# Reordering a software-pipelined loop: an x tile, a v1 sum, result copies and the gate's turn change places with roundings, packings and matmul blocks

## The reference, cut to what matters

```
y  = layernorm over channels(x)
ca = sigmoid(mlp(mean over positions(y)) + mlp(max over positions(y)))     # channel gate
y  = y * ca
s  = conv7x7([mean over channels(y), max over channels(y)])                # token gate
t  = x + y * sigmoid(s)                                                    # attention, then as tokens
h  = bitlinear(layernorm(t), w1)      # x rounded to 8 bits by its row maximum, w to -1, 0, 1
h  = gelu(h)
t  = t + bitlinear(h, w2)             # h rounded the same way
```

## Time and profile before

| | us |
|---|---|
| median of 3 runs | 318.17 (317.60 to 318.43) |
| the profiled execution, device time | 317.06 |
| its span in the profile | 315.2 |
| PE busy | 272.2 (86%) |
| DVE busy | 247.3 (78%) |
| ACT busy | 218.0 (69%) |
| POOL busy | 161.4 (51%) |

### The profile page before, as it was taken

One profiled execution on the slowest core, in us unless ns is written; L12 is line 12 of the kernel. 1 busy time (PEld: TensorE's weight loads), 2 busy tenths in 40 slices (PEclk: granted clock), 3 DMA queues, 4 the chain that ended last, 5 costly groups with the idle time before them and its releaser, 6 DMA issues.

```text
span 315.2 us, 5808 instructions
## 1 busy us (share of the span) xinstructions
PE 272.2 (86%) x1834; PEld 154.7 (49%) x1834; DVE 247.3 (78%) x558; ACT 218.0 (69%) x442; POOL 161.4 (51%) x256
## 2 busy tenths in 40 slices
PE   2557768496999999999999999999999998999974
PEld 2344645363455355635563556355636553554431
DVE  0756979879699969896989698969896988798410
ACT  2287398478486877687768776877687758777731
POOL 7404355316855385538553855385538553455410
PEclk9755758879699999999999999999999999999998
DMA  5899400003073049403840384049405630263493
GB/s 133 308 380 423 156 1 2 0 0 65 5 166 70 8 62 231 105 6 63 225 111 6 61 223 113 5 65 224 113 3 66 166 71 15 54 168 74 79 215 100
DMA packets 71077, 34.19 MB, mean 108 GB/s; under 512 B 52040, under 2 KB 68424, under 8 KB 70536
## 3 DMA queue, kind: packets, MB, share of 16 engines
q1 hardware_dynamic: 69384, 32.78, 41.5%
q10 hardware_dynamic: 1664, 1.05, 1.2%
HBM read 14.94 MB, written 6.29 MB: 67 GB/s over the span
## 4 chain that ended last, share of the span: by engine, by line
PE 52%; DVE 15%; POOL 13%; issue 8%; ACT 7%; DMA 3%; SPq 1%; ACTq 0%; POOLq 0%; DVEq 0%
PE ps_o L1153 17%; PE ps_h L1142 9%; PE ps_t L1142 9%; POOL v L451 5%; PE front L1073 4%; POOL w_room L474 3%; PE front L1063 3%; PE ps_t L1184 2%; POOL rs L445 2%; DVE pv L782 2%; ACT junk L520 2%; PE small L1089 2%; DVE w_room L884 2%; DVE t L814 2%; PE front L1162 2%
## 5 line engine op out<-in xcount | busy, mean ns | idle before, releaser
L1153 PE MATMUL ps_o<-w2T,hq 128*128 128x512 f16 x384 | 92.7, 380 | 1.2 <-DMA hq<-w_raw 1.2
L474 POOL TENSOR_SCALAR w_room<-w_room,q 128x1024 f32<-128x1024 f32 x48 | 59.3, 1247 | 54.3 <-DVE q L851 54.3
L841 DVE TENSOR_REDUCE amax<-w_room 128x1 f32<-128x1024 f32 (+1 forms) x48 | 57.2, 1208 | 2.2 <-ACT w_room L520 2.2
L1153 PEld LDWEIGHTS ps_o<-w2T,hq 128*128 128x128 f16 x384 | 35.4, 98 | 37.3 <-issue 3.6
L1142 PE MATMUL ps_h<-w1T,xq 128*128 128x512 f16 x208 | 52.3, 394 | 1.1 <-ACT xq L520 0.8
L520 ACT ACTIVATE w_raw<-w_room 128x1024 f16<-128x1024 f16 x48 | 50.1, 1048 | 0.6 <-POOL w_room L474 0.6
L520 ACT ACTIVATE w_room<-ps_h,s 128x512 f32<-128x512 f32 x52 | 35.0, 689 | 13.0 <-PE ps_h L1142 11.9
L1142 PE MATMUL ps_t<-w1T,xq 128*128 128x512 f16 x176 | 43.3, 384 | 0.0
L520 ACT ACTIVATE w_room<-ps_t,s 128x512 f32<-128x512 f32 x44 | 30.2, 687 | 8.4 <-PE ps_t L1142 8.3
L520 ACT ACTIVATE junk_m<-front 128x192 bf16<-128x192 f32 x64 | 20.5, 329 | 17.8 <-DVE pooled L757 17.7
L1142 PEld LDWEIGHTS ps_h<-w1T,xq 128*128 128x128 f16 x208 | 19.2, 100 | 23.2 <-issue 2.4
(11 more groups left out here) (121 smaller groups left out, 459.5 us busy)
## 6 DMA issues: line engine op xcount, KB each, us to landing
out<-w_room SPq DMA_DIRECT2D x16, 384.0 KB, 3.4
x_in<-in_x SPq DMA_DIRECT2D x14, 384.0 KB, 5.6
w_room<-in_L_ffn_w SPq DMA_DIRECT2D x4, 1024.0 KB, 8.7
w_raw<-in_L_ffn_w SPq DMA_DIRECT2D x4, 1024.0 KB, 12.1
x_in<-in_x ACTq DMA_DIRECT2D x2, 384.0 KB, 3.7
hq<-w_raw SPq DMA_TRANSPOSE x48, 3.2
fc_raw<-in_L_conv_fc_w ACTq DMA_DIRECT2D x2, 128.0 KB, 4.2
taps_rev<-in_L_conv_sa_w SPq DMA_DIRECT2D x2, 0.2 KB
```

Source lines behind the costliest of these rows:

```text
L474: pool.tensor_scalar(part, part, q2[tile.par][:, 0:1], MAGIC, ALU.mult, ALU.add).then_inc(g_rounded, 1)
L841: chain.mark(dve.tensor_reduce(amax2[:, i:i + 1], w1_room[:, first + i * F // 2:first + (i + 1) * F // 2 + i], AX.X, ALU.max, apply_absolu ...
L1153: last = pe.matmul(ps_o[:, :], hq[tile.par][:, k, :], w2T[:, k, :], start=(k == 0), stop=(k == NF - 1))
```

## The change

Four functions of the loop are reordered. No arithmetic is added or removed. One wait is added.

- POOL: `normalise1(fresh, 2)` moves from the end of the body to ahead of the last `round_g`, that of tile (nxt, 1), directly behind `normalise1(fresh, 0, 1)`.
- PE: `turn_x(fresh, 2)` moves ahead of `turn_xq(nxt, 2)` and the last quarter of `ffn_out(pair, 2)`. `turn_ca(att)` moves from behind the third block of `ffn_in(nxt, 1)` to behind the second.
- ACT: `pack_g` now packs one half at a time. At the body's start the second half of (pair, 1) goes behind `token_mean(att, 0)`. In the middle the second half of (pair, 2) goes behind `token_mean(att, 3)`. At the end `copy_out(pair, 1)` goes ahead of `sum_channels(att, 2)`, `copy_x(fresh, 2)` ahead of `copy_xq(nxt, 2)`, and the second half of (nxt, 0) to the very end. `copy_caT` moves one block of `gelu` forward.
- ACT: `gelu` waits before block 2 until the packings of the tile two before are done.

```
@@ POOL body
                     if turn and s == NT - 1:
                         normalise1(pair.plus(3), 0, 1)
+                        normalise1(pair.plus(3), 2)
                     if normalise or s < NT - 2:
                         round_g(Tile(pair, s + 2))
-                if turn:
-                    normalise1(pair.plus(3), 2)
@@ ACT gelu
+                    if b == 2:
+                        wait(act, g16_ready, tile.at(2, -2))
@@ ACT body
-                pack_g(Tile(pair, 1), Tile(pair.plus(-1), 2) if pair.c > 0 else None, OUT_BANK[0])
+                pack_g(Tile(pair, 1), 0)
+                if pair.c > 0:
+                    copy_out(Tile(pair.plus(-1), 2), OUT_BANK[0])
                 if attend:
                     token_mean(att, 0, V1_BANK[0])
+                pack_g(Tile(pair, 1), 1)
+                if attend:
                     token_mean(att, 1, V1_BANK[1])
...
-                pack_g(Tile(pair, 2), Tile(pair, 0), OUT_BANK[1])
+                pack_g(Tile(pair, 2), 0)
+                copy_out(Tile(pair, 0), OUT_BANK[1])
                 if attend:
                     token_mean(att, 3, V1_BANK[3])
+                pack_g(Tile(pair, 2), 1)
...
-                    gelu(Tile(nxt, 1), blocks=(0, 1, 2))
+                    gelu(Tile(nxt, 1), blocks=(0, 1))
                 if attend:
                     copy_caT(att)
                 if normalise:
-                    gelu(Tile(nxt, 1), blocks=(3,))
+                    gelu(Tile(nxt, 1), blocks=(2, 3))
                 if attend:
                     sum_channels(Tile(att, 0))
                     sum_channels(Tile(att, 1))
                 if normalise:
-                    pack_g(Tile(nxt, 0), halves=(0,))
+                    pack_g(Tile(nxt, 0), 0)
+                copy_out(Tile(pair, 1), OUT_BANK[2])
                 if attend:
                     sum_channels(Tile(att, 2))
-                copy_out(Tile(pair, 1), OUT_BANK[2])
-                if normalise:
-                    pack_g(Tile(nxt, 0), halves=(1,))
-                if normalise:
-                    copy_xq(Tile(nxt, 2), XQ_BANK[2])
                 if turn:
                     copy_x(Tile(fresh, 2), X_BANK[2])
+                if normalise:
+                    copy_xq(Tile(nxt, 2), XQ_BANK[2])
+                    pack_g(Tile(nxt, 0), 1)
@@ PE body
-                    ffn_in(Tile(nxt, 1), blocks=(0, 1, 2))
+                    ffn_in(Tile(nxt, 1), blocks=(0, 1))
                 if attend:
                     turn_ca(att)
                 if normalise:
-                    ffn_in(Tile(nxt, 1), blocks=(3,))
+                    ffn_in(Tile(nxt, 1), blocks=(2, 3))
...
                 ffn_out(Tile(pair, 2), (1, 2))
+                if turn:
+                    b = turn_x(Tile(fresh, 2), X_BANK[2], b)
                 if normalise:
                     a = turn_xq(Tile(nxt, 2), XQ_BANK[2], a)
                 ffn_out(Tile(pair, 2), (3,))
-                if turn:
-                    b = turn_x(Tile(fresh, 2), X_BANK[2], b)
```

More of the change, by code:

```diff
@@ L575, in gelu, with pack_g @@
                          scale=s1[tile.pair.par][:, tile.s:tile.s + 1])
-            def pack_g(tile, out_tile=None, out_bank=None, halves=range(2)):
+            def pack_g(tile, half):
                 if tile.at() < 2:
                     act.wait_ge(w_turned, 10)
[L582 to L588, removed]
+                cols = slice(half * F // 2, (half + 1) * F // 2)
+                wait(act, g_rounded, tile.at(2, half + 1))
+                wait(act, h_turned[tile.par][half], tile.turns(-1))
+                copy(g16[tile.par][:, cols], low_halves(g[tile.par][:, cols]), g16_ready, bias=-F16_ZERO)
             def copy_out(tile, bank):
@@ L655, in _ @@
             gelu(Tile(pair0, 1), None, h_start, (2, 3))
-            pack_g(Tile(pair0, 0))
+            pack_g(Tile(pair0, 0), 0)
+            pack_g(Tile(pair0, 0), 1)
             copy_x(Tile(pair2, 0), 1)
@@ L697, in body @@
                 if normalise:
-                    pack_g(Tile(nxt, 0), halves=(0,))
+                    pack_g(Tile(nxt, 0), 0)
+                copy_out(Tile(pair, 1), OUT_BANK[2])
                 if attend:
                     sum_channels(Tile(att, 2))
-                copy_out(Tile(pair, 1), OUT_BANK[2])
-                if normalise:
-                    pack_g(Tile(nxt, 0), halves=(1,))
+                if turn:
+                    copy_x(Tile(fresh, 2), X_BANK[2])
                 if normalise:
                     copy_xq(Tile(nxt, 2), XQ_BANK[2])
-                if turn:
-                    copy_x(Tile(fresh, 2), X_BANK[2])
+                    pack_g(Tile(nxt, 0), 1)
             for c in range(NP):
```

## The result

The changed kernel takes 321.68 us (median of 4, 320.57 to 323.0) against 317.88 us for the kernel before: a ratio of 1.012, 95% interval 1.0067 to 1.0172, so it is slower by 3.8 us, 1.2%. The profiled execution took 322.66 us with a span of 320.8, against 317.06 and 315.2.

The account below looks back on a forecast made before the run. PE's own order bounds the kernel, busy 30.37 of 31.54 us per body. Losses of 5 x 1.52 less gains of 6 x 0.35 and 6 x 0.48 give +2.6 us: 320.8 us, own range 319.6 to 322.0, whole range 316.9 to 323.6.

Parts of the forecast that it names:

- The end gains 0.48 and half of the stall becomes a new wait: Body's end on PE: conv starts at 205.68 instead of 206.16, held by DVE's split statistics; gain 0.48 us, not 0.91.
- POOL's chain, step by step: Start of next body: POOL's v1, round_g and 1/sigma wait for the aggregate behind conv; L830 comes 1.52 us late.
- the rule that the prediction names: DVE and GpSimd lock a shared SBUF port exclusively, the second fully blocked; mere bandwidth splitting would make the sum about +1.4.
- No slack on the way to PE: Start of body: nothing hides L830's lateness; PE's turn_xq(nxt, 0) at +8.74 instead of +7.50, turn_v1(att, 2) 1.52 us late.
- `fc1` gives 0.35 back: Middle of body: last token_mean ahead of a packing on ACT removes fc1's wait, gaining 0.35 us in bodies 0 to 5.
- In body 5 ... I take the same 0.48: End of body 5, without turn_x: the result copy also comes forward, so the same 0.48 us gain was assumed.
- bodies 6 and 7 "don't change": Bodies 6, 7 and the last DMA-bound stretch were forecast unchanged, 0 us.
- The sum: Whole kernel: 5 x 1.52 - 6 x 0.35 - 6 x 0.48 = +2.6 us, 320.8 us on the median.
- x comes late: Rival, chance 0.16: x's load, with 0.25 us slack, stalls PE 0.45 us in bodies 1 to 4; +1.8, 322.6 us.
- POOL slips through: Rival, chance 0.22: POOL's L446 gets ahead of DVE's L814, L830 only 0.77 us late; sum -1.1, 317.0 us.

Follow-up runs that it names:

- the end's edits alone: Kernel before with only PE's turn_x and ACT's copy_out, copy_x and last packing moved at the body's end, plus gelu's wait: 318.53 us, single execution.
- the second profile: The changed kernel, unaltered, measured again beside new runs of the kernel before: 321.81 us, ratio 1.0112.
- the channel sum's experiment: Changed kernel, but in body 5 alone ACT's sum_channels(att, 2) stands ahead of copy_out again: 320.07 us, ratio 1.0069.
- the aggregate first: Changed kernel with DVE's aggregate(fresh, 2) ahead of sum_conv(att): 318.29 us, ratio 1.0005; with body 5's channel sum also ahead of copy_out: 315.98 us.
- the best one: Changed kernel with aggregate ahead of sum_conv, body 5's channel sum ahead of copy_out, and 1/sigma between round_g's halves: 310.56 us, again 310.58 us.

## Why the prediction was right, and where it was not

- **The end gains 0.48 and half of the stall becomes a new wait.** Right: 0.54 in the changed kernel and 0.44 with the end's edits alone, `conv` held by the split with 0.22 us of idle time. That the body-end edits alone then gain nothing (31.54 us) the forecast had not said, but it follows from its reason: POOL's chain of v1, `round_g`, v1 and 1/sigma ends last.
- **POOL's chain, step by step.** From the body's start, forecast and measured: L444 +0.57, +0.53; end of L446 +2.0, +2.01; L451 +2.15, +2.12; `round_g` +2.95, +2.88; L834 +6.68, +6.51. L446 was caught by L818 (the old L814) as L444 had been in the earlier trace rows: it takes 0.69 us and ends with it. Wrong in one detail: it was not POOL that paid for the meeting with the old L826. POOL's half started 0.07 us ahead of it, so DVE waited and its row grew from 0.51 to 1.33 us. That cost nothing, since 1/sigma came later still, but it shortened L834's wait to 1.51 us, where 1.8 to 2.4 were forecast. POOL's idle time was forecast from S - 1.2 on and began at S - 0.39, since v1 of tiles 0 and 1 (L451 at 206.60, 1.54 us) ended only then. L446 grew by 0.50 us to the end of L818, as by the rule that the prediction names, and not by half of that.
- **No slack on the way to PE.** Right: `turn_xq` at +8.59 (forecast +8.74, before +7.50), `ffn_in(nxt, 0)` 1.35 to 1.4 us late (forecast 1.52).
- **`fc1` gives 0.35 back.** The stretch from `ffn_in` to `ffn_in` is 0.29 us shorter (10.57 against 10.86), by itself and in the changed kernel alike. By itself 0.07 of it is lost again at the body's end, so that a body gains 0.22 (31.32 against 31.54). A little too high.
- **"In body 5 ... I take the same 0.48", and bodies 6 and 7 "don't change".** This is the step that failed. The forecast took the cover of the later channel sum from a middle body, where DVE splits some 0.4 us after the sum ends (the accumulator is read by 206.30, L799 starts at 206.72), and used it for body 5, where DVE has no statistics of a fresh tile to take and is early. It said that without cover the sum would cost what it comes late. It comes 0.23 us late and PE waits 1.41 us, for POOL's halves of g start in that gap: the body's end is 0.96 us longer than before instead of 0.48 shorter. Another 1.69 us (1.25 in the second profile) are lost behind it at half clock, a cost that the forecast did not have. With the sum put back both disappear (the channel sum's experiment, and again with the aggregate first).
- **The sum.** In the profiled pair the middle bodies were forecast 0.1 to 0.16 us too slow each (0.6 in four), and bodies 5 and 6 were 3.0 us too fast. By the medians 2.6 us stand against 3.8. That 320.8 us comes so near to the measured 321.68 is in part luck: a loss priced too high in the middle bodies stands against one that was missed in bodies 5 and 6, and the profiled executions differ by 5.6 us where the medians differ by 3.8 (that of the kernel before was shorter than all its timed runs, that of the changed kernel one of the two longer of its four). Where the other executions are shorter no profile shows.
- **x comes late.** The slack of 0.25 us was about right: no row of the changed kernel's loop shows a wait for x. Body 4 is 0.1 us (0.3 in the second measurement) longer than the others. In three faster versions PE waited for x, in body 4 only: 0.32 us with the aggregate first, 0.19 with body 5's sum put back as well, 0.26 and 0.19 in the two profiles of the best one. Body 4 is 0.41 to 0.56 us longer there than the bodies before it.
- **POOL slips through.** It did not, in any of the profiles of this order.

What stays open: the half clock behind the wait. It began 0.2 to 2.3 us after the wait had ended and lasted some 3.4 us. Of the kernels with the 1.4 us wait at the end of body 5, five profiles have it there and one (the end of the body only) does not. Of the five waits of 1.45 to 1.49 us in the profile of POOL's move alone, one was followed by it. No profile shows it behind the waits of 1.23 to 1.30 us in the changed kernel's middle bodies, nor in any kernel's bodies 1 to 6 without such waits (body 0 starts at half clock in all of them). So the wait is needed for it here, as far as these runs go, and is not enough.

## What to carry to other kernels

A move on one in-order queue is priced by everything that then stands behind its wait, and by who else asks for that queue's next result: here v1 came earlier, as was wanted, and 1/sigma 1.35 us later, as nobody wanted. When the moved wait can't be avoided, look for the small thing in the queue that others need, and place it first: 0.8 us of POOL's work between two halves turned a kernel that was 1.2% slower into one that is 0.8% faster, and with two more such orders (the aggregate first, body 5's sum put back) 2.4% faster. And price each boundary body of a pipelined loop from its own rows: what covers an operation in the middle bodies may be absent in the last ones.

## What the runs showed of the hardware

- When DVE and POOL meet, the one that comes second is held until about the end of the other's instruction, either way round. POOL's L446 took 0.69 us instead of 0.19 behind DVE's L818; DVE's L830 took 1.33 instead of 0.51 behind POOL's L474. The worst case is small: DVE's L799 and L800, six numbers a row, took 1.00 and 1.06 us, each waiting for one of POOL's two halves of 1.1 us, since POOL's second half was ready to start when DVE had finished its first operation. The Trainium skill states in "SBUF — State Buffer", section "Who interferes with whom", that issue order and not the shape of the operation decides who blocks. These rows agree in that either engine can be the one that is held. They don't give the order to better than about 0.1 us: in the kernel before, L796 started 0.06 us behind POOL's L474 (267.11 and 267.05) and still took its 0.17 us.
- The granted clock fell to half for some 3.4 us behind an idle stretch of 1.4 us in an otherwise busy loop, in six of eleven cases, and cost 1.25 to 1.7 us each time. Where it happened, the wait cost about twice its length.
- A wait may be listed as "issue": the earlier trace rows put PE's 0.24 us in front of `fc1` down to that, and it went away when ACT's mean came earlier.
